# Narrow attention on one Trainium2 core: two heads stacked in 64-row tiles, regrouped loads, splits on GpSimd, division in token layout

## The chip, the cores and the metric

One core of a Trainium2 chip runs the whole program. TensorE (PE) does matmuls from SBUF into the eight banks of PSUM, VectorE (DVE), ScalarE (ACT) and GpSimd (POOL) work on 128 partitions, and SyncE (SP) issues the DMA transfers of this kernel. Each engine runs its own list of instructions in order and waits on semaphores. The metric is the device time of one execution in microseconds.

## What is computed

The reference runs a network of 16 layers on x of 4 x 512 x 128, each added to x after a layer norm. Two layers are "narrow attention": 16 heads of 8 features, without a mask (L0b) and with a causal one (L2b). Cut to what matters:

```python
q = heads(x @ Wq.T + bq); k = heads(x @ Wk.T + bk); v = heads(x @ Wv.T + bv)   # [B, 16, 512, 8]
s = einsum('bhqd,bhkd->bhqk', q, k) * scale          # L2b: -inf where key > query
out = (softmax(s) @ v).reshape(B, 512, 128) @ Wo.T + bo
```

The scores must be as exact as float32. The kernel gets that from bf16 matmuls: q and k are each split into three bf16 parts (value, rest, rest of the rest), and the six products of parts that matter are stacked along the contraction.

## The kernel before

The outer loop runs twice, over two batch elements (b = 0, 1) at a time; the layers stand in it one after the other, each a `Stage` with a list for each engine. Activations are kept feature-major: 128 features on partitions, 512 tokens along a row. `narrow_attention` (L1167) is one stage, so it runs four times: L0b and L2b in each pass.

A stage begins with the layer norm (`Norm`, banks 0 to 3). PE projects q and k (L1260, L1261) and v (L1263) into banks 0, 1, 2, for b = 0 and then for b = 1 into the same banks. DVE adds the biases (L1386, L1387) and splits into parts in five steps (L1389 to L1397) for b = 0, and again for b = 1 after `parted` says that the first parts have left. SP sends the parts of a batch element to memory in one transfer of 128 rows (`send_parts`, L1225) and loads them back (`stack`, L1232, L1233), since the heads must change partitions: operands `qs` and `ks` hold six groups of 8 rows for each head and ones or zeros below; row 48 and the next two of `qs` take the negative row maximum in three parts. Before, one head fills a 128-row operand (only 51 rows are not constant). GpSimd fills `qs` and `ks` whole (L1365), then builds `vpad`, v with a column of ones next to each head (L1367 to L1375).

The work of a stage is cut into 8 units of 4 heads (u = 4b + i). A unit has 17 "top" steps: 16 score tiles (4 heads x 4 query tiles) that PE makes (`top_scores`, L1278, with a mask matmul L1281 in L2b) into banks 4 and 5 in turn, each reduced by DVE to a row maximum (`maxima`, L1403), and a transpose of the maxima (L1273), which DVE negates (L1411) and splits in five more steps (L1413 to L1421). SP puts the three parts into `qs` (L1246) and only then, when they have landed, loads unit u + 2 and waits for it. Units 0 and 1 are loaded ahead (`AHEAD` = 2).

A unit then has 8 slots. In slot s PE makes transposed scores of two heads (`scores`, L1294, mask L1297) into banks 0 and 1 or 2 and 3, ACT takes the exponential of both (L1356) into `pt`, and after each second slot PE multiplies by `vpad` (`products`, L1309; four column tiles of 32) into bank 6 or 7. Between them PE does the tops of later units: `LEAD` = 25 tops run before slot 0, and 17 in each 8 slots afterwards, by `tops_before`. All waits are in the order of the list: a top that must wait for its load (`stacked`) holds up all that follows on PE.

After two units ACT copies a bank of sums (L1349), PE spreads each head's denominator over its 8 rows with a matmul (`spread_den`, L1316), and DVE takes the reciprocal of 128x512 (L1427), multiplies (L1429) and adds v's bias (L1431). The last stretch multiplies by Wo (L1335) for both batch elements and adds to x (L1443).

## Time and profile before

| | us |
|---|---|
| median of 3 runs (lowest, highest) | 3660.25 (3659.43, 3673.93) |
| the profiled execution | 3659.59 |
| its span, from first to last instruction | 3657.6 |
| PE busy | 2741.8 (75%) |
| DVE busy | 1890.3 (52%) |
| ACT busy | 1451.8 (40%) |
| POOL busy | 558.9 (15%) |
| DMA queue of SP | 45.93 MB in 31328 packets, 4.8% of 16 engines' time |

Busy times are sums over the whole span, and a matmul's end is modelled, so a busy PE isn't PE at its peak. They are averages over sixteen layers with different limits; what narrow attention costs is read from windows over its stages and the timeline inside them. The TensorE clock is granted at one of two levels, 1.2 or 2.4 GHz; rows give it as a share of the higher one (0.50 or 1.00), and stretches as a mean.

### The profile page before, as it was taken

What the parts mean: (1) busy time and instruction counts of PE and PEld (TensorE: products, weight loads), DVE (VectorE), ACT (ScalarE), POOL (GpSimd) and SP (SyncE); (2) the same over time, 40 slices, a digit from 0 to 9 for tenths busy, and PEclk for the clock granted to TensorE, in tenths of its full rate; (3) what the DMA queues carried; (4) which work ended last, traced back from release to release, by engine and by line L of the source; (5) the groups of instructions that cost most, each with busy time, mean ns of one, the idle gap of its engine ahead of it and who ended that gap; (6) DMA issues with size and microseconds to landing.
All of it is one profiled execution on the core that took longest, in us unless ns stands there. A gap on an engine that the chain in (4) does not pass through costs nothing. (4 is left out here: it accounts for less than half of the span.)

```text
span 3657.6 us, 33867 instructions
## 1 busy us (share of the span) xinstructions
PE 2741.8 (75%) x12082; PEld 1218.6 (33%) x12082; DVE 1890.3 (52%) x2639; ACT 1451.8 (40%) x2368; POOL 558.9 (15%) x324
## 2 busy tenths in 40 slices
PE   3565769899878579466746657789997877894677
PEld 1221145445344234123212211554443433341232
DVE  4867642455122751595649586415552237416955
ACT  2442511555234244343524424125552433443434
POOL 0533000000003101161006320000000040011600
PEclk8897977999989799799968979689999898997999
DMA  2001000000010210000000020000000102100000
GB/s 91 0 1 39 15 0 1 1 1 1 0 46 1 44 50 6 0 1 1 1 13 0 0 43 11 1 1 1 1 1 0 46 9 41 51 0 0 0 1 6
DMA packets 31504, 48.18 MB, mean 13 GB/s; under 512 B 7520, under 2 KB 19808, under 8 KB 31328
## 3 DMA queue, kind: packets, MB, share of 16 engines
q1 hardware_dynamic: 31328, 45.93, 4.8%
q8 instruction: 98, 1.61, 0.2%
q14 instruction: 78, 0.64, 0.1%
HBM read 38.18 MB, written 7.34 MB: 12 GB/s over the span
## 5 line engine op out<-in xcount | busy, mean ns | idle before, releaser
L1598 ACT ACTIVATE L1b_pr<-ps,L1b_mneg 128x512 f32<-128x512 f32 x256 | 173.8, 684 | 195.7 <-DVE L1b_mneg L1637 195.7
L518 POOL TENSOR_TENSOR xs<-xs,L2f_part 128x512 f32<-128x512 f32 x32 | 40.5, 1264 | 1287.6 <-DVE L2f_part L507 1287.6
L1356 ACT ACTIVATE L0b_pt<-ps 128x1024 f32<-128x1024 f32 x128 | 129.6, 1024 | 209.4 <-PE ps L1294 209.4
L1635 DVE TENSOR_REDUCE L1b_m<-ps 128x2 f32<-128x1024 f32 x128 | 156.7, 1224 | 105.0 <-PE ps L1502 101.0
...
L1403 DVE TENSOR_REDUCE L0b_mx<-ps 128x1 f32<-128x512 f32 x256 | 161.2, 684 | 47.7 <-PE ps L1278 45.0
L1046 POOL TENSOR_TENSOR L0a_db<-L0a_du,L0a_bs 128x1024 f32<-128x1024 f32 x64 | 150.3, 2353 | 227.8 <-ACT L0a_bs L1017 217.1
L1046 POOL TENSOR_TENSOR L3a_db<-L3a_du,L3a_bs 128x1024 f32<-128x1024 f32 x64 | 150.3, 2353 | 226.5 <-ACT L3a_bs L1017 216.0
L1356 ACT ACTIVATE L2b_pt<-ps 128x1024 f32<-128x1024 f32 (+3 forms) x128 | 88.4, 704 | 204.2 <-PE ps L1297 203.7
L1278 PE MATMUL ps<-L0b_ks,L0b_qs 128*128 128x512 bf16 x256 | 104.0, 446 | 87.0 <-DMA L0b_ks<-parts_dram 51.8
L1661 DVE COPY L1b_prt<-ps 128x512 f32<-128x512 f32 x128 | 88.5, 691 | 125.0 <-PE ps L1513 124.7
L1122 DVE TENSOR_TENSOR_SCAN L0a_hs<-ps,L0a_db 128x1024 f32<-128x1024 f32 x64 | 146.1, 2283 | 9.9 <-ACT ps L1009 8.0
L1122 DVE TENSOR_TENSOR_SCAN L3a_hs<-ps,L3a_db 128x1024 f32<-128x1024 f32 x64 | 146.1, 2282 | 9.8 <-ACT ps L1009 8.0
L1403 DVE TENSOR_REDUCE L2b_mx<-ps 128x1 f32<-128x128 f32 (+3 forms) x256 | 116.7, 486 | 54.0 <-PE ps L1281 52.4
L1502 PE MATMUL ps<-L1b_k,L1b_q 64*128 64x512 f32 x512 | 144.0, 640 | 0.0
L1525 PE MATMUL ps<-L1b_prt,L1b_v 128*64 128x512 f32 x512 | 136.7, 614 | 4.1 <-issue 2.0
L1513 PE MATMUL ps<-weights,L1b_pr 128*128 128x128 f32 x1024 | 135.8, 275 | 3.0 <-ACT L1b_pr L1598 3.0
L1278 PE MATMUL ps<-L2b_ks,L2b_qs 128*128 128x128 bf16 (+3 forms) x256 | 80.1, 347 | 76.5 <-DMA L2b_ks<-parts_dram 50.2
L1513 PEld LDWEIGHTS ps<-weights,L1b_pr 128*128 128x128 f32 x1024 | 115.6, 141 | 50.6 <-issue 43.5
L507 DVE SCALAR_TENSOR_TENSOR L2f_part<-ps,weights,L2f_masks 128x512 f32<-128x512 f32 x32 | 24.0, 751 | 205.7 <-PE ps L439 205.7
L946 PE MATMUL ps<-L0a_hc,weights 128*128 128x512 f32 x256 | 127.7, 623 | 2.7 <-DVE L0a_hc L1127 2.7
L507 DVE SCALAR_TENSOR_TENSOR L2g_part<-ps,weights,L2g_masks 128x512 f32<-128x512 f32 x32 | 24.0, 751 | 203.7 <-PE ps L439 203.7
...
## 6 DMA issues: line engine op xcount, KB each, us to landing
...
```

The lines of the kernel that those rows point to most:

```text
L946: mm = pe.matmul(g.ps[:, k, :], g.w("ident"), hc[:, n % 2, k, :], start=(s == 0), stop=(s == NS - 1))
L1046: pool.tensor_tensor(db[:, n % 2, :, :], du[:, b, :, :], bcast(bs[:, n % 2, :], 1, 2), ALU.mult).then_inc(input_ready, 1)
L1122: dve.tensor_tensor_scan(flat(hs), decay_banks(n).rearrange("p k t -> p (k t)"), flat(db), 0.0, ALU.mult, ALU.add).then_inc(scanned, 1)
L1278: mm = pe.matmul(g.ps[:, 4 + a % 2, 0:span(t)], qs[:, b, i, r, t * P:(t + 1) * P], ks[:, b, i, r, 0:span(t)], start=True, stop=not causal)
L1356: act.activation(pt[:, n % 3, 2 * half:2 * half + 2, q0:T], g.ps[:, 2 * (s % 2):2 * (s % 2) + 2, q0:T], ACT.Exp).then_inc(prob, 1)
L1403: dve.tensor_reduce(mx[:, u, n:n + 1], g.ps[:, 4 + a % 2, 0:span(n % 4)], AX.X, ALU.max).then_inc(top_in, 1)
L1502: mm = pe.matmul(g.ps[:, 2 * (s % 2) + h, :], q[HE * h:HE * h + HE, u % 3, t * P:(t + 1) * P], k[HE * h:HE * h + HE, u % 3, :], start=True ...
L1513: mm = pe.transpose(g.ps[:, 4 + h, j * P:(j + 1) * P], pr[:, s % 2, h, j * P:(j + 1) * P], g.w("ident"))
L1525: mm = pe.matmul(g.ps[HE * h:HE * h + HE, PV, :], v[:, u % 4, j, HE * h:HE * h + HE], prt[:, u % 2, h, j, :], start=(j == 0), stop=(j == K ...
L1598: act.activation(pr[:, s % 2, h, :], g.ps[:, 2 * (s % 2) + h, :], ACT.Exp, bias=mneg[:, s % 2, h:h + 1], accum_out=total[:, u % 2, t, h:h ...
L1635: dve.tensor_reduce(m[:, s % 2, :], g.ps[:, 2 * (s % 2):2 * (s % 2) + 2, :], AX.X, ALU.max).then_inc(max_raw, 1)
L1661: dve.tensor_copy(prt[:, u % 2, 0, :, t * P:(t + 1) * P], g.ps[:, 4, :].rearrange("p (j c) -> p j c", c=P)).then_inc(turned_dve, 1)
```

## The change

Two heads share one operand: head 1 on rows 0 to 63, head 2 on rows 64 to 127, 50 rows of each used. `qs` and `ks` become half as large, a score matmul contracts 64 rows, and the two heads of a slot stand in the two halves of the array. The mask matmuls of L2b keep their full height; in `scores` both come after both score matmuls. The negative maximum has two parts instead of three.

Projections of q and k come out with their heads permuted (in `_pack`), b = 1 gets banks of its own (3, 6, 7), and PE starts on b = 0 when its norm is done. DVE splits only b = 0; GpSimd splits b = 1 and, for every unit, the maxima. GpSimd fills `qs` and `ks` through f32 views, and waits for DVE's split before it fills `vpad`.

The parts leave in six transfers for a batch element (part x tensor) into a memory layout of two blocks of 64 rows. A unit's load has again 12 transfers, but with rows of 2 KB and groups of 3, 2 and 1 stacked parts, some of which repeat the source with a step of zero. SP sends the parts of b = 1 after the maxima of unit 0 and ahead of the load of unit 2. `LEAD` is 28. Maxima are collected in an order by halves.

The division moves: PE transposes the copied sums (`turn`), DVE takes reciprocals of 32 columns and multiplies 256, PE transposes back (`turn_back`), and ACT adds the bias (`take_at`). The output of b = 0 moves from the end into slot 41.

The core of the diff:

```diff
-Q_PART = (0, 0, 1, 1, 0, 2)
-K_PART = (0, 1, 0, 1, 2, 0)
+Q_PART = (0, 0, 0, 1, 1, 2)
+K_PART = (0, 1, 2, 0, 1, 0)
...
-    LEAD = 25
+    LEAD = 28
...
+                def send(b, part):
+                    if b == 0:
+                        sp.wait_ge(cut_dve, part + 1)
+                    else:
+                        sp.wait_ge(cut_pool, part + 1)
+                    for x in range(2):
+                        sp.dma_start(g.parts_dram[b, part, x, :, :, :].rearrange("q c t -> c q t"), cut[:, b, part, x, :]).then_inc(sent[part], 16)
+
+                def load(u):
                     b, i = u // 4, u % 4
...
+                    for j, n in ((0, 3), (3, 2), (5, 1)):
+                        for r in range(2):
+                            rows = slice(HALF * r + DH * j, HALF * r + DH * (j + n))
+                            src = g.parts_dram[b, :, :, 16 * i + 8 * r:16 * i + 8 * r + 8, :, :]
+                            sp.dma_start(qs[rows, b, 2 * i:2 * i + 2, :], bcast(src[Q_PART[j], 0], 0, n)).then_inc(stacked, 16)
+                            sp.dma_start(ks[rows, b, 2 * i:2 * i + 2, :], src[K_PART[j]:K_PART[j] + n, 1]).then_inc(stacked, 16)
...
                 for u in range(UN):
...
+                    send_max(u)
+                    if u == 0:
+                        for part in range(PARTS):
+                            send(1, part)
                     if u + AHEAD < UN:
...
+                        load(u + AHEAD)
+                        sp.wait_ge(stacked, (u + AHEAD + 1) * LOADS)
+                    sp.wait_ge(m_rows, 64 * (u + 1))
...
+                    c, t, r = n // 8, n // 2 % 4, HALF * (n % 2)
+                    mm = pe.matmul(g.ps[:, 4 + a % 2, 0:span(t)], qs[r:r + HALF, b, 2 * i + c, t * P:(t + 1) * P],
+                                   ks[r:r + HALF, b, 2 * i + c, 0:span(t)], start=True, stop=not causal)
...
+                    dve.reciprocal(inv[:, :, :], rows[:, :, :, DH]).then_inc(inverse, 1)
...
+                    dve.tensor_tensor(att[:, :, :, 0:DH], rows[:, :, :, 0:DH], bcast(inv[:, :, :], 3, DH), ALU.mult).then_inc(scaled, 1)
...
-        g.parts_dram = nc.dram_tensor("parts_dram", [NB, P, 3, 2, T], BF16, kind="Internal").ap()
+        g.parts_dram = nc.dram_tensor("parts_dram", [NB, 3, 2, P // 2, 2, T], BF16, kind="Internal").ap()
```

SP's queue in the first L0b, from the last load of unit 1 to the first load of unit 2, before (a name is out<-in, then the shape written; waits in brackets):

```order
L1233 DMA L0b_ks<-parts_dram 8x4x512
L1225 DMA parts_dram<-L0b_cut 128x3072 [waits L0b_cuts,L0b_stacked]
L1246 DMA L0b_qs<-L0b_mcut 1x16x128 [waits L0b_m_steps,L0b_ones_in,L0b_parted]
L1246 DMA L0b_qs<-L0b_mcut 1x16x128 x2
L1233 DMA L0b_qs<-parts_dram 8x4x512 [waits L0b_m_rows]
L1233 DMA L0b_ks<-parts_dram 8x4x512
```

and now:

```order
L1236 DMA L0b_ks<-parts_dram 8x1024
L1244 DMA L0b_qs<-L0b_mcut 1x8x128 [waits L0b_m_hi,L0b_stacked]
...
L1244 DMA L0b_qs<-L0b_mcut 1x8x128 [waits L0b_m_lo]
...
L1227 DMA parts_dram<-L0b_cut 2x64x512 [waits L0b_cut_pool]
...
L1227 DMA parts_dram<-L0b_cut 2x64x512 [waits L0b_cut_pool]
...
L1227 DMA parts_dram<-L0b_cut 2x64x512 [waits L0b_cut_pool]
...
L1235 DMA L0b_qs<-parts_dram 24x1x1024
L1236 DMA L0b_ks<-parts_dram 24x1x1024
```

The one 128x3072 transfer of b = 1, which stood ahead of the maxima, is now six of 2x64x512 between the maxima of unit 0 and the load of unit 2.

PE from slot 0 of the first L0b (L1294 is a score, L1278 a top, L1309 products, L1273 the transpose), before:

```order
L1294 MATMUL ps<-L0b_qs,L0b_ks 128x512 [waits L0b_m_rows]
L1294 MATMUL ps<-L0b_qs,L0b_ks 128x512
L1278 MATMUL ps<-L0b_ks,L0b_qs 128x512 [waits L0b_top_in] x3
L1294 MATMUL ps<-L0b_qs,L0b_ks 128x512 x2
L1278 MATMUL ps<-L0b_ks,L0b_qs 128x512 [waits L0b_top_in] x2
L1294 MATMUL ps<-L0b_qs,L0b_ks 128x512 [waits L0b_prob]
L1294 MATMUL ps<-L0b_qs,L0b_ks 128x512
L1309 MATMUL ps<-L0b_pt,L0b_vpad 32x512 [waits L0b_vpad_ready,L0b_prob]
...
L1278 MATMUL ps<-L0b_ks,L0b_qs 128x512 [waits L0b_top_in] x2
L1294 MATMUL ps<-L0b_qs,L0b_ks 128x512 [waits L0b_prob]
...
L1278 MATMUL ps<-L0b_ks,L0b_qs 128x512 [waits L0b_top_in]
L1273 MATMUL ps<-weights,L0b_mx 16x128 [waits L0b_top_in]
```

and now (L1309 a score, L1293 a top, L1327 products, L1288 the transpose):

```order
L1309 MATMUL ps<-L0b_qs,L0b_ks 128x512 [waits L0b_m_rows,L0b_v_in,L0b_proj_in]
L1309 MATMUL ps<-L0b_qs,L0b_ks 128x512
L1293 MATMUL ps<-L0b_ks,L0b_qs 128x512 [waits L0b_top_in] x3
L1309 MATMUL ps<-L0b_qs,L0b_ks 128x512 x2
L1293 MATMUL ps<-L0b_ks,L0b_qs 128x512 [waits L0b_top_in] x2
L1309 MATMUL ps<-L0b_qs,L0b_ks 128x512 [waits L0b_prob]
L1309 MATMUL ps<-L0b_qs,L0b_ks 128x512
L1327 MATMUL ps<-L0b_pt,L0b_vpad 32x512 [waits L0b_vpad_ready,L0b_prob]
...
L1288 MATMUL ps<-weights,L0b_mx 16x128 [waits L0b_top_in]
L1293 MATMUL ps<-L0b_ks,L0b_qs 128x512 [waits L0b_stacked,L0b_top_in]
L1309 MATMUL ps<-L0b_qs,L0b_ks 128x512 [waits L0b_prob]
...
L1293 MATMUL ps<-L0b_ks,L0b_qs 128x512 [waits L0b_top_in] x2
```

The transpose of unit 1's maxima and, right behind it, the first top of unit 2 with its wait for `stacked` now stand in slot 2; before, the transpose ended slot 3, and that top stood in slot 4.

DVE at the end of unit 0's maxima, before:

```order
L1403 TENSOR_REDUCE L0b_mx<-ps 128x1 [waits L0b_top] x16
L1411 TENSOR_SCALAR L0b_mt<-ps 16x128 [waits L0b_top]
L1413 CAST L0b_mcut<-L0b_mt 16x128 [waits L0b_top_in]
L1415 TENSOR_TENSOR L0b_mt<-L0b_mt,L0b_mcut 16x128 [waits L0b_m_steps]
L1417 CAST L0b_mcut<-L0b_mt 16x128 [waits L0b_m_steps]
L1419 TENSOR_TENSOR L0b_mt<-L0b_mt,L0b_mcut 16x128 [waits L0b_m_steps]
L1421 CAST L0b_mcut<-L0b_mt 16x128 [waits L0b_m_steps]
L1403 TENSOR_REDUCE L0b_mx<-ps 128x1 [waits L0b_top] x16
```

DVE now:

```order
L1467 TENSOR_REDUCE L0b_mx<-ps 128x1 [waits L0b_top] x16
L1471 TENSOR_SCALAR L0b_mt<-ps 16x128 [waits L0b_top]
L1467 TENSOR_REDUCE L0b_mx<-ps 128x1 [waits L0b_top] x16
L1471 TENSOR_SCALAR L0b_mt<-ps 16x128 [waits L0b_top]
...
L1471 TENSOR_SCALAR L0b_mt<-ps 16x128 [waits L0b_m_lo,L0b_top]
```

and GpSimd now, in the same stage (fills, one step of the split of b = 1, unit 0's maxima):

```order
L1409 MEMSET L0b_ks 128x4096
L1411 MEMSET L0b_vpad 128x4096 [waits L0b_cut_dve]
...
L1426 CAST L0b_cut<-L0b_ln_sq 128x1024 [waits L0b_proj_in]
L1429 TENSOR_TENSOR L0b_ln_sq<-L0b_ln_sq,L0b_cut 128x1024 [waits L0b_cut_pool]
...
L1435 CAST L0b_mcut<-L0b_mt 16x128 [waits L0b_top_in]
L1437 TENSOR_TENSOR L0b_mt<-L0b_mt,L0b_mcut 16x128 [waits L0b_m_hi]
L1439 CAST L0b_mcut<-L0b_mt 16x128 [waits L0b_m_rest]
```

The five small steps have left DVE, and GpSimd has them behind its split of b = 1.

## Rows read from the trace of the kernel before

**Rows 1.** one row a stretch: length, busy us of each engine (instructions), granted clock, DMA share, GB/s
```profile
271.70:469.70 198.00, 133.02 (x568) 34.97 (x568) 139.61 (x208) 72.77 (x77) 36.88 (x11) 0.86 0.12 25
...
1170.00:1342.80 172.80, 112.21 (x824) 50.58 (x824) 115.87 (x208) 52.15 (x77) 36.85 (x11) 0.85 0.14 29
```

**Rows 2.** the same view, inside the first L0b stage
```profile
331.40:441.40 110.00, 88.81 (x427) 22.08 (x425) 83.89 (x151) 55.04 (x56) 0.00 (x0) 0.95 0.14 22
...
441.40:458.80 17.40, 12.81 (x76) 2.98 (x72) 4.86 (x5) 10.87 (x12) 0.00 (x0) 1.00 0.01 2
...
458.80:469.90 11.10, 6.41 (x10) 2.23 (x10) 5.95 (x5) 0.60 (x1) 0.00 (x0) 0.85 0.00 0
```

**Rows 3.** timeline: start us, length us, engine, line, operation [idle before <-what ended it]
```profile
285.69 7.35 POOL L1365 MEMSET L0b_qs<- 128x8192 bf16 x1
...
287.47 6.11 DVE L1393 CAST L0b_cut<-L0b_ln_xc 128x1024 bf16<-128x1024 f32 x1
...
304.30 0.33 SPq L1233 DMA_DIRECT2D L0b_qs<-parts_dram  x1
...
307.98 0.77 DVE L1393 CAST L0b_cut<-L0b_ln_xc 128x1024 bf16<-128x1024 f32 x1
...
311.90 1.01 PE L1278 MATMUL ps<-L0b_ks,L0b_qs 128*128 128x512 bf16 x2 [25.80 <-DMA L0b_ks<-parts_dram]
```

**Rows 4.** DMA view: a send, 12 loads, three row loads (301:304.3, 304:311.8, 325.5:328.9)
```profile
DMA packets 144, 0.79 MB, mean 238 GB/s; under 512 B 16, under 2 KB 16, under 8 KB 144
...
DMA packets 480, 0.39 MB, mean 50 GB/s; under 512 B 96, under 2 KB 480, under 8 KB 480
...
DMA packets 96, 0.01 MB, mean 4 GB/s; under 512 B 96, under 2 KB 96, under 8 KB 96
```

**Rows 5.** windows of 1 us: 2 KB writes, 1 KB reads twice, 2 KB reads (last columns)
```profile
1837.00:1838.00 1.00, 0.00 (x0) 0.00 (x0) 0.00 (x0) 0.00 (x0) 0.00 (x0) 0.62 0.89 350
...
306.30:307.30 1.00, 0.00 (x0) 0.00 (x0) 0.97 (x2) 0.00 (x0) 1.00 (x2) 0.50 0.31 87
...
308.30:309.30 1.00, 0.00 (x0) 0.00 (x0) 0.96 (x2) 0.00 (x0) 0.71 (x1) 0.50 0.58 66
...
1042.50:1043.50 1.00, 1.00 (x2) 0.50 (x2) 0.28 (x1) 0.37 (x1) 0.00 (x0) 0.50 0.84 313
```

**Rows 6.** timeline of PE, L0b: two products one cycle apart
```profile
428.68 1.06 PE L1309 MATMUL ps<-L0b_pt,L0b_vpad 128*32 128x512 f32 x8
...
432.21 1.07 PE L1309 MATMUL ps<-L0b_pt,L0b_vpad 128*32 128x512 f32 x8
```

**Rows 7.** timeline of PE, L0b: the transpose of the maxima
```profile
424.53 0.27 PE L1273 MATMUL ps<-weights,L0b_mx 128*16 128x128 f32 x1 [0.90 <-DVE L0b_mx L1403]
```

**Rows 8.** timeline of PE, L0b: products after PE had been idle
```profile
380.68 1.94 PE L1309 MATMUL ps<-L0b_pt,L0b_vpad 128*32 128x512 f32 x8
```

**Rows 9.** timeline of ACT, L0b: exponentials of two slots without tops
```profile
448.44 1.94 ACT L1356 ACTIVATE L0b_pt<-ps 128x1024 f32<-128x1024 f32 x2 [0.78 <-PE ps L1294]
```

**Rows 10.** timeline of PE, L1b: full-height and 64-row f32 matmuls
```profile
682.37 1.13 PE L1488 MATMUL ps<-xn,weights 128*128 128x512 f32 x2
...
683.34 1.04 PE L1513 MATMUL ps<-weights,L1b_pr 128*128 128x128 f32 x8
...
684.30 1.13 PE L1502 MATMUL ps<-L1b_k,L1b_q 64*128 64x512 f32 x4
...
685.36 1.08 PE L1525 MATMUL ps<-L1b_prt,L1b_v 128*64 128x512 f32 x4
```

**Rows 11.** groups of instructions by form: out<-in xcount, busy us, mean ns, idle before
```profile
L1427 DVE RECIPROCAL xn<-ps 128x512 f32<-128x512 f32 x16 | 53.7, 3355 | 49.1 <-PE ps L1316 49.1
...
L1666 DVE RECIPROCAL L1b_inv<-L1b_total 128x8 f32<-128x8 f32 x32 | 6.2, 193 | 0.0
```

**Rows 12.** timeline of SP, L2b: row-maxima issues of two units
```profile
1236.18 2.02 SPq L1246 DMA_DIRECT2D L2b_qs<-L2b_mcut  x3
...
1248.42 1.77 SPq L1246 DMA_DIRECT2D L2b_qs<-L2b_mcut  x3
```

More of the change, by code:

```diff
@@ new lines, in send_max @@
+                def send_max(u):
+                    b, i = u // 4, u % 4
+                    for p, ready in enumerate((m_hi, m_lo)):
+                        sp.wait_ge(ready, u + 1)
+                        for r in range(2):
+                            row = HALF * r + ROWS + p
+                            sp.dma_start(qs[row:row + 1, b, 2 * i:2 * i + 2, :].rearrange("o c (t k) -> o (c t) k", k=P),
+                                         mcut[8 * r:8 * r + 8, u % 2, p, :]).then_inc(m_rows, 16)
@@ new lines, in _ @@
+                for part in range(PARTS):
+                    send(0, part)
+                sp.wait_ge(filled, 2)
+                for part in range(PARTS):
+                    sp.wait_ge(sent[part], 32)
+                load(0)
+                sp.wait_ge(stacked, LOADS)
+                load(1)
+                sp.wait_ge(stacked, 2 * LOADS)
+                for u in range(UN):
+                    send_max(u)
+                    if u == 0:
+                        for part in range(PARTS):
+                            send(1, part)
+                    if u + AHEAD < UN:
+                        if u + AHEAD == 4:
+                            for part in range(PARTS):
+                                sp.wait_ge(sent[part], 64)
+                        load(u + AHEAD)
+                        sp.wait_ge(stacked, (u + AHEAD + 1) * LOADS)
+                    sp.wait_ge(m_rows, 64 * (u + 1))
@@ L1434, in _, with output @@
+                def output(b):
+                    dve.wait_ge(out_ready, b + 1)
+                    dve.scalar_tensor_tensor(out=g.xs[:, b, :], in0=g.ps[:, 7, :], scalar=g.w(w + "_bo"), in1=g.xs[:, b, :],
+                                             op0=ALU.add, op1=ALU.add).then_inc(added, 1)
+                for a in range(LEAD):
                     maxima(a // 17, a % 17)
-                for s in range(8 * UN):
+                for s in range(SLOTS):
                     for a in range(tops_before(s), tops_before(s + 1)):
@@ L1438, in _ @@
                     if s % 16 == 4 and s > 16:
-                        normalise(s // 16 - 1)
-                normalise(2 * NB - 1)
-                for b in range(NB):
-                    dve.wait_ge(out_ready, b + 1)
-                    dve.scalar_tensor_tensor(out=g.xs[:, b, :], in0=g.ps[:, b, :], scalar=g.w(w + "_bo"), in1=g.xs[:, b, :],
-                                             op0=ALU.add, op1=ALU.add).then_inc(added, 1)
+                        divide(s // 16 - 1)
+                    if s == 42:
+                        output(0)
+                divide(2 * NB - 1)
+                output(NB - 1)
 def wide_attention(g, name):
@@ L2086, in by_pairs @@
         out = np.zeros((4, 2, 2, 8, 2, m.shape[1]), f)
[L2087 removed]
+        out[:, :, 0] = np.asarray(m).reshape(2, 2, 4, 8, -1).transpose(2, 1, 3, 0, 4)
         return out.reshape(128, -1)
```

275 lines of the change are left out of this document (141 added, 134 removed).

## Prediction, made before the changed kernel had run

> **What bounds the kernel now.** I read the windows over whole stages first, then inside one stage the timeline of PE and DVE, then the DMA view. The change touches only `narrow_attention`, which runs four times: L0b and L2b, in each of two passes of the outer loop. One L0b takes 198.0 us, one L2b 172.8 us [rows 1], together 742 of the 3657.6 us span. The other stages keep their instructions, so I sum differences inside these four against the profiled 3659.6 us (span 3657.6 plus 2.0 around it; the median of the runs is 3660.25, so no correction between them). Inside L0b no engine is full; there are four regimes.
> (a) An opening up to the first score tile: the first matmul on stacked operands starts only at 311.90, after 25.80 us of PE idleness that a DMA ends [rows 3]. Most of it is DVE's six-step split, whose casts take 6.11 us while GpSimd fills `qs` and `ks` (7.35 us a piece) and 0.77 us when it doesn't.
> (b) 53 slots with "tops" (score tiles made only for the maxima) in them, 331.4 to 441.4 [rows 2]. Products start 3.52 to 3.53 us apart (428.68, 432.21) [rows 6]. Two tops (0.43 until the reduce starts), two reduces of 0.62, a wake-up and top of 0.35, a score pair of 0.5 and products of 1.0 make that loop: PE and DVE take turns.
> (c) Slots without tops: two exponentials of 1.94 us together plus 0.78 us waiting for scores, 2.72 us for two slots [rows 9].
> (d) A tail of 11 us [rows 2] with a reciprocal of 3.36 us [rows 11] and output matmuls.
>
> **The change: the loads.** Here lies the decision. A transfer ends with small packets, one for each share it is dealt into. In before, 12 loads of shape 8x4x512 (32 rows of 1 KB each) show 480 packets, 96 of them under 512 B: 384 rows and 8 closing packets for each load. The 128x3072 send shows 144, so 16 closing ones. Three 1x16x128 row loads show 96: 48 rows and 16 each [rows 4]. So a transfer is cut along its outermost dimension of more than one element, into at most 16 shares, and not along its rows. Both sides must be cut alike. The new sends write 2x64x512 into memory: two shares. The new loads read an outer dimension of 3, 2 or 8. Hence all parts of a batch element pass through two of sixteen engines: 3 parts x 2 tensors x 64 rows of 1 KB = 384 packets on each. That the same two serve every send is assumed; rival 1 holds the other reading.
> The Trainium skill ("DMA: Bandwidth & Descriptors", section on why a DMA increments its semaphore by 16) gives it as a rule: the count of engines is the largest up to 16 that divides the slowest dimension of both sides, and the lowest-numbered ones are taken. By that rule the 8 and 16 of the trace come out, and the new sends get 2 engines.
> How long is a 1 KB packet? Nearest are writes of 2 KB rows to memory: 350 GB/s on 16 engines at 0.89 busy, 0.89 x 16 x 2048 / 350000 = 83 ns, so 42 ns for 1 KB if size is all. Reads of 1 KB rows take 0.31 x 16 x 1024 / 87000 = 58 ns in the first microseconds and 0.58 x 16 x 1024 / 66000 = 144 ns when queued [rows 5]. I take 50 ns, nearest to the writes; range 42 to 80, with 144 as the far end. So the parts of one batch element take 384 x 0.050 = 19.2 us, against some 3 us for the 128-row send.
> A load: engine 0 gets 4 x (8 + 8 + 1) = 68 packets of 2 KB. 2 KB reads cost 0.84 x 16 x 2048 / 313000 = 88 ns [rows 5]; since reads slow when queued I take 110: 7.5 us, plus 0.9 to start and 1.2 to be seen, 9.6 us. Before: first issue 304.30 to the first matmul 311.90, 7.6 less 0.1, so 7.5 [rows 3].
>
> **Opening.** GpSimd's fills halve and end before the casts, so DVE has part 0 at 281.9 and part 2 at 286.1 instead of 301.0. But engines 0 and 1 start at 282.8 and end at 302.0; the loads start at 303.2 (before 304.3), the first top at 312.8 (+1.0). LEAD 28 adds three tops of 0.7 us: the first score is 3.1 us late.
>
> **The stall.** SP issues: row maxima of unit 0, the sends of batch element 1, then the load of unit 2, and waits for it. The maxima of unit 0 are ready some 12.5 us after the first top, at 325.3; with GpSimd's three small steps and four issues of 0.59 the sends go out at 327.7. They end at 328.6 + 19.2 = 347.8, and the load queued behind them on the same engines at 347.8 + 7.5 + 1.2 = 356.5. PE wants unit 2's first top (number 34) in slot 2, 5.2 us after the first score at 333.4: 338.6. It is in order, so scores and products stand behind it: 17.8 us. In L2b the slot comes 5.7 us after its first score, the maxima sooner: 19.5 us. After idleness PE is granted the low clock (1.2 GHz): products take 1.94 us instead of 1.06 [rows 6, 8], and a cycle costs 2 us more: +3 for one to two cycles. GpSimd's own split of batch element 1 (five steps from about 295; each moves less than the 16 KB a partition that a fill writes in 7.35 us [rows 3], so 5 us at most) is over by 320 and holds no send up. Behind the waiting SP stand the row maxima of unit 1, 3 us later on, hidden by slots 3 to 7.
>
> **Steady slots.** An f32 matmul stands as two instructions in these rows: one of full height (x2) takes 1.13 us, and two of 64 rows (x4) take 1.13 us together [rows 10], so a score pair costs half: 3.52 - 0.22 = 3.30 us a cycle. The five small DVE steps move away, but before they ran beside products and cost PE nothing beyond the 0.90 us wait for the transpose [rows 7]; with LEAD 28 the transpose stands behind products and that wait goes: that cycle is 2.96. A unit in L0b: 3.30 + 3.30 + 3.90 (one extra top) + 2.96 = 13.5 instead of 15.3 us. 53 slots took 111.1 us; now 51/8 x 13.5 = 86.1, plus 2 x 2.6 for turning, dividing and turning back, plus 2.3 for the first output moved into slot 41: 93.6, a gain of 17.5. Reciprocals of 32 columns instead of 512 lie near the 0.19 us row, not 3.36 [rows 11]. Slots without tops: 13 x 1.24 + 2.1 = 18.2 instead of 17.3, +0.9. Tail: copy 0.7, turn 1.2, divide 0.9, turn back 1.2, bias 0.75, output matmuls 1.9 to 3.6, add 0.85, so 8 instead of 10.9: -2.9.
> L0b: +3.1 + 17.8 + 3 - 17.5 + 0.9 - 2.9 = **+4.4 us**.
> In L2b each top is a 64-row matmul and then a full-height mask. From a full-height f32 matmul to what follows is 683.34 - 682.37 = 0.97 us, from a 64-row pair 685.36 - 684.30 = 1.06 [rows 10]: 0.09 for a change of tiling, at most, and 44 changes a unit are 4 us, nothing if hidden. I take 2. Score pairs give 1.1, the transpose 0.7: a unit 12.4 to 12.5 instead of 12.24 (SP rows 1236.18 to 1248.42) [rows 12]; bounds 12.0, where SP's own loop of 2.4 + 9.6 us stands, and 14.5. 94.7 us become 51/8 x 12.5 + 7.5 = 87.2, -7.5; slots without tops +3.7; tail -1.7.
> The Trainium skill ("TensorEngine Tiling (Array Packing)", key properties) says that a change of mode drains the array, which speaks against this change; by that rule all 4 us would be paid, 13 us more for each L2b. The 0.09 us row doesn't show more.
> L2b: +3.1 + 19.5 + 3 - 7.5 + 3.7 - 1.7 = **+20.1 us**.
> Sum: 2 x (4.4 + 20.1) = +49, 3659.6 + 49 = **3709 us**.
>
> **Rivals.** (1) The sends spread over all engines, as the SBUF side's 128 rows would allow; this ends on the other side. The parts land about 3 us after the last issue, the load takes 7.5: the first score is 12.9 us early, the stall 1 to 3 us, no clock loss. L0b -12.9 + 1.2 - 17.5 + 0.9 - 2.9 = -31.2, L2b -12.9 + 3 - 7.5 + 3.7 - 1.7 = -15.4, twice: 3566 us. For it: no row shows two sides with different outer counts. Against: the 8x4x512 loads had 32 rows on both sides and used 8. It decides by engines: the sum is zero when a batch element's sends take 49/8 = 6.1 us less, 13 us; two engines at 42 ns need 16.
> (2) Packets slower than I take, as queued reads are: each 10 ns is 3.84 us x 2 x 4 stages = 31 us; 80 ns gives 3801, 144 gives about 4000. For it, that the second pair of rows 5 shows just this slowing; against, that those are reads.
> (3) The 64-row bf16 tiles don't overlap, or the change of tiling is paid in full: 0.88 us a unit in each stage, 5.6 x 4 = +22, and +13 x 2 for the drains: 3755.
>
> **Numbers.** Forecast 62%: 3709, own range 3675 to 3755 (42 to 57 ns a packet, steady slots 5 us a stage either way). Rival 1 16%, rival 2 12%, rival 3 10%. The range 3640 to 3800 leaves out rival 1 and a little above. Half a per cent, about what a measurement of this kernel can tell from no change, is 18 us. Faster takes rival 1 and a low tail of the forecast, 0.18; same is the part of the forecast with packets at 42 ns and better slots, 0.15; slower 0.67.
>
> **What would show it.** The six sends of a stage carry 2 closing packets each and engines move under 55 GB/s for about 19 us; PE's row for the first top ends its wait near 25 us as before; one idle time of 16 to 20 us ended by a load stands in each stage in slot 2; score pairs take about 0.4 us for two; GpSimd's three small steps hide; units come 13.5 us apart in L0b. Wrong if sends land in 3 us, if the stall is absent or much longer, or if L2b's units run far from 12.5 us.

## The result, and the profile after

The changed kernel takes 3716.7 us (median of 4 runs, 3697.2 to 3721.1), the kernel before 3659.8 us beside it: ratio 1.014, 95% interval 1.009 to 1.018. It is slower by 1.4%, 57 us, where 49 were forecast. The profiled execution took 3715.9 us with a span of 3714.2.

First the windows over the four stages, columns as in [rows 1]; of before, [rows 1] shows the first two, and the third and fourth are as long, 197.4 and 173.2 us.

```profile
270.31:464.64 194.33, 120.67 (x592) 29.65 (x592) 97.14 (x159) 75.15 (x81) 28.50 (x39) 0.81 0.08 25
1170.05:1378.87 208.82, 158.83 (x848) 56.78 (x848) 78.02 (x159) 55.07 (x81) 28.50 (x39) 0.67 0.07 24
2127.18:2318.80 191.62, 116.79 (x592) 28.61 (x592) 97.13 (x159) 75.17 (x82) 28.51 (x39) 0.83 0.08 26
3019.03:3211.83 192.80, 141.56 (x848) 54.30 (x848) 77.57 (x159) 55.03 (x81) 28.51 (x39) 0.76 0.08 26
```

L0b is 4 to 6 us *shorter* than before, L2b 36 us longer in the first pass and 20 in the second. The granted clock in L2b fell from 0.85 to 0.67 and 0.76. The four stages together give +45.7 us; 10.9 us more lie in stages whose instructions did not change.

The sends and the stall, in the timeline of SP and PE (first L0b, which starts at 270.31):

```profile
280.36 10.55 SPq L1227 DMA_DIRECT2D parts_dram<-L0b_cut  x6
...
299.22 0.76 SPq L1235 DMA_DIRECT2D L0b_qs<-parts_dram  x1
...
308.72 0.61 PE L1293 MATMUL ps<-L0b_ks,L0b_qs 64*128 64x512 bf16 x2 [27.06 <-DMA L0b_ks<-parts_dram]
...
324.44 10.67 SPq L1227 DMA_DIRECT2D parts_dram<-L0b_cut  x6
335.15 2.64 SPq L1235 DMA_DIRECT2D L0b_qs<-parts_dram  x1
...
349.66 0.58 PE L1293 MATMUL ps<-L0b_ks,L0b_qs 64*128 64x512 bf16 x1 [15.31 <-DMA L0b_ks<-parts_dram]
```

SP issues six sends from 280.4 on, and they have landed by 299.2, when it goes on to the load. The same happens again from 324.4, and PE sits idle for 15.31 us until unit 2's load, queued behind them, lands. The DMA view of 280.3 to 299.2 (the six sends), then of 299.2 to 308.65 (one unit's load):

```profile
DMA packets 780, 0.79 MB, mean 42 GB/s; under 512 B 12, under 2 KB 780, under 8 KB 780
...
q1 hardware_dynamic: 780, 0.79, 12.2%
...
DMA packets 244, 0.39 MB, mean 42 GB/s; under 512 B 52, under 2 KB 52, under 8 KB 244
```

12 closing packets for six sends are two each: two engines. Two of sixteen busy is 12.5%; the row says 12.2%. A packet of 1 KB takes 0.122 x 16 x 18.9 / 768 = 48 ns. The load's 52 closing packets are 4 x 3 + 4 x 2 + 4 x 8, as its outermost dimensions of 3, 2 and 8 give.

The issue of 10.67 us isn't even. The first three sends of the second six take 0.55, 0.54 and 0.88 us to issue, the next three 3.22, 2.63 and 2.63, and the first transfer of the load behind them 2.64 (335.15), where 0.76 was enough with nothing ahead of it (299.22). So the full queue of two engines holds SP up as well. From 335.15 to the top that waits, 14.5 us pass, against 9.5 for the load that had the engines to itself.

In L0b products now come 3.30 us apart (3.53 in [rows 6]) and row maxima 13.43 us apart (PE, then SP):

```profile
366.50 1.07 PE L1327 MATMUL ps<-L0b_pt,L0b_vpad 128*32 128x512 f32 x8
...
369.80 1.07 PE L1327 MATMUL ps<-L0b_pt,L0b_vpad 128*32 128x512 f32 x8
...
365.59 2.72 SPq L1244 DMA_DIRECT2D L0b_qs<-L0b_mcut  x4
...
379.02 2.73 SPq L1244 DMA_DIRECT2D L0b_qs<-L0b_mcut  x4
```

In L2b the same issues, 12.24 us apart in [rows 12], stand 20 to 22 us apart and then 13.65; the windows of the same stretch (PEclk is the third number from the right) show why:

```profile
1270.98 2.73 SPq L1244 DMA_DIRECT2D L2b_qs<-L2b_mcut  x4
1291.45 2.73 SPq L1244 DMA_DIRECT2D L2b_qs<-L2b_mcut  x4
1313.63 2.73 SPq L1244 DMA_DIRECT2D L2b_qs<-L2b_mcut  x4
1327.28 2.72 SPq L1244 DMA_DIRECT2D L2b_qs<-L2b_mcut  x4
...
1260.00:1270.00 10.00, 10.00 (x48) 2.87 (x47) 4.19 (x9) 3.25 (x4) 0.00 (x0) 0.50 0.02 7
...
1300.00:1310.00 10.00, 10.00 (x52) 3.51 (x44) 3.85 (x9) 3.08 (x5) 0.00 (x0) 0.50 0.06 18
...
1320.00:1330.00 10.00, 9.82 (x74) 4.05 (x74) 5.26 (x13) 5.08 (x7) 0.98 (x3) 1.00 0.11 31
```

For 64 us after the stall in the first pass PE is busy 10 us of 10 and still granted half its clock (0.50, 1.2 GHz). At full clock it is busy 9.8 of 10: PE, not SP or DVE, bounds L2b now. One unit at full clock, before (between the two issues of [rows 12]) and after:

```profile
1236.18:1248.42 12.24, 10.57 (x97) 4.89 (x97) 8.57 (x23) 5.53 (x8) 0.00 (x0) 1.00 0.21 34
```
```profile
1313.63:1327.28 13.65, 13.47 (x102) 5.54 (x100) 7.89 (x18) 6.06 (x9) 0.98 (x4) 0.99 0.10 31
```

PE was busy 10.57 of 12.24 us and is busy 13.47 of 13.65.

The rows of PE around a mask say what fills it; three of after, then three of before, both at full clock:

```profile
1320.29 0.23 PE L1293 MATMUL ps<-L2b_ks,L2b_qs 64*128 64x128 bf16 x1
1320.45 0.23 PE L1296 MATMUL ps<-cb 128*128 128x128 bf16 x1
1320.61 0.28 PE L1293 MATMUL ps<-L2b_ks,L2b_qs 64*128 64x256 bf16 x1
```
```profile
1237.85 0.23 PE L1278 MATMUL ps<-L2b_ks,L2b_qs 128*128 128x128 bf16 x1
1237.91 0.22 PE L1281 MATMUL ps<-cb 128*128 128x128 bf16 x1
1237.99 0.28 PE L1278 MATMUL ps<-L2b_ks,L2b_qs 128*128 128x256 bf16 x1
```

From a 64-row top to its full-height mask 0.16 us pass, where two full-height tiles stand 0.06 apart; from the mask to the next top 0.16 against 0.08. So a change of tiling costs 0.08 to 0.10 us each way.

### The profile page after: what moved, and what is told of

Read it like the earlier page. It is cut to its first block and busy times, and to the rows that moved or that the text cites. A ratio compares the mean times of both kernels' runs of the same rounds, so it can differ in the third digit from the quotient of the medians.

```text
span 3714.2 us, 34111 instructions
## 1 busy us (share of the span) xinstructions
PE 2804.3 (76%) x12170; PEld 1223.3 (33%) x12178; DVE 1728.4 (47%) x2443; ACT 1464.7 (39%) x2384; POOL 525.5 (14%) x436
## 5 line engine op out<-in xcount | busy, mean ns | idle before, releaser
L1467 DVE TENSOR_REDUCE L2b_mx<-ps 128x1 f32<-128x128 f32 (+3 forms) x256 | 122.8, 490 | 167.9 <-PE ps L1296 162.9
L1293 PE MATMUL ps<-L0b_ks,L0b_qs 64*128 64x512 bf16 x256 | 100.2, 449 | 122.9 <-DMA L0b_ks<-parts_dram 85.4
L1293 PE MATMUL ps<-L2b_ks,L2b_qs 64*128 64x128 bf16 (+3 forms) x256 | 96.3, 376 | 84.5 <-DMA L2b_ks<-parts_dram 82.2
L116 PE MATMUL ps<-xs,weights 128*128 128x512 f32 x128 | 79.6, 754 | 73.4 <-PEq L220 27.4
L946 PE MATMUL ps<-L3a_hc,weights 128*128 128x512 f32 x256 | 131.0, 636 | 2.7 <-DVE L3a_hc L1127 2.7
L946 PE MATMUL ps<-L0a_hc,weights 128*128 128x512 f32 x256 | 126.8, 619 | 2.7 <-DVE L0a_hc L1127 2.7
```

The costliest lines, as they stand in the source:

```text
L946: mm = pe.matmul(g.ps[:, k, :], g.w("ident"), hc[:, n % 2, k, :], start=(s == 0), stop=(s == NS - 1))
L1293: mm = pe.matmul(g.ps[:, 4 + a % 2, 0:span(t)], qs[r:r + HALF, b, 2 * i + c, t * P:(t + 1) * P], ks[r:r + HALF, b, 2 * i + c, 0:span(t)], ...
L1467: dve.tensor_reduce(mx[:, u, col:col + 1], g.ps[:, 4 + a % 2, 0:span(n // 2 % 4)], AX.X, ALU.max).then_inc(top_in, 1)
```

## The experiments

Stage lengths, from windows between the table loads that bound each stage (L0b, L2b of the first pass, then of the second), and medians; "before" ran beside each and took 3659 to 3662 us.

| kernel | L0b | L2b | L0b | L2b | median us | ratio (95%) |
|---|---|---|---|---|---|---|
| before | 198.2 | 173.0 | 197.4 | 173.2 | 3660 | |
| after | 194.3 | 208.8 | 191.6 | 192.8 | 3716.7 | 1.014 (1.009-1.018) |
| spread | 175.1 | 187.1 | 174.5 | 178.1 | 3636.6 | 0.993 (0.990-0.995) |
| order2 | 186.1 | 190.4 | 181.3 | 190.2 | 3667.4 | 1.001 (1.000-1.003) |
| nomask | 194.8 | 178.0 | 194.6 | 188.5 | 3668.0 | 1.001 (1.000-1.002) |
| spread_order_nomask | 170.8 | 161.1 | 167.9 | 160.8 | 3583.0 | 0.978 (0.976-0.980) |
| order2_halfmask | 181.9 | 171.9 | 184.7 | 171.3 | 3631.1 | 0.992 (0.989-0.995) |
| before_nomask | 197.2 | 171.0 | 197.2 | 169.8 | 3656.4 | 0.999 (0.998-1.000) |
| before_two | 227.9 | 215.0 | 226.6 | 214.9 | 3805.5 | 1.039 (1.037-1.041) |
| loads18 | 164.2 | 145.0 | 164.3 | 150.5 | 3542.3 | 0.968 (0.965-0.971) |
| loads18_mask | 164.3 | 159.3 | 164.2 | 159.3 | 3564.1 | 0.974 (0.972-0.977) |
| loads18_halfmask | 164.1 | 148.3 | 164.2 | 149.8 | 3544.4 | 0.967 (0.965-0.969) |
| loads18_lead24 | 163.6 | 165.8 | 163.6 | 165.8 | 3583.6 | 0.979 (0.977-0.981) |
| loads18_dvemax | 168.5 | 147.5 | 168.3 | 146.5 | 3556.3 | 0.971 (0.969-0.973) |

### The sends over sixteen engines: spread

```
-sp.dma_start(g.parts_dram[b, part, x, :, :, :].rearrange("q c t -> c q t"), cut[:, b, part, x, :])
+for c in range(2):
+    sp.dma_start(g.parts_dram[b, part, x, :, c, :], cut[HALF * c:HALF * (c + 1), b, part, x, :])
```

> The changed kernel with one edit: each 2x64x512 send becomes two sends of 64x512, so that the outermost dimension has 64 elements on both sides. Theory A (the time of the sends is set by the two engines they are dealt over): 2 closing packets per send become 16, the 17 us from first send to last landing become 4 to 6 us, the first top matmul comes 11 to 13 us earlier in each of the four stages, and PE's idle time of 15.3 us (L0b) and 14.0 us (L2b) in slot 2 shrinks to 0 to 4 us. That is 4 x (12 + 12) = 96 us less than 3717, so about 3620, and 3590 if the stretch of low granted clock in L2b (60 us of it after the stall in the first pass) is a sequel of the stall. Rival B (the sends are bound by the issue on SP's queue, 10.6 us for six): the new sends issue just as slowly, gain 4 x 5 or less, 3690 or more. On the clock: theory C (low clock in L2b is a sequel of the stall) has units 2 to 4 of L2b at about 13.7 us; rival D (it comes from the work itself: 64-row tops with a full-height mask behind each) has L2b at the low clock for as long as before, units of 20 to 21 us.

Measured 3636.6 us, 80 less than after. The timeline of PE shows the opening 10 us shorter and the stall halved:

```profile
300.22 0.60 PE L1294 MATMUL ps<-L0b_ks,L0b_qs 64*128 64x512 bf16 x2 [17.13 <-DMA L0b_ks<-parts_dram]
...
333.30 0.58 PE L1294 MATMUL ps<-L0b_ks,L0b_qs 64*128 64x512 bf16 x1 [7.57 <-DMA L0b_ks<-parts_dram]
```

Theory A holds in kind; a stall of 6 to 8 us stays because SP still issues twelve sends, at 0.6 us each and 7.5 in all, ahead of the load. The sum closes: SP's issue of the sends is 3.1 us shorter than in the changed kernel, and from the load's first issue to the waiting top 9.8 us pass instead of 14.5; together 7.8 us, and the stall fell by 7.7. The clock went against theory C in the first pass: with the stall at 6 us, L2b's units were still 21.4, 20.5 and 16 us long. In the second they were 21.4 and then 13.8, as in the changed kernel.

### Two engines in the kernel before: before_two

```
-sp.dma_start(g.parts_dram[b], cut[:, :, :, :])                       # 128 rows outermost
+sp.dma_start(g.parts_dram[b].rearrange("q c a x t -> c q (a x t)"), cut[...])   # 2 x 64
```

> The kernel before the change with one part of the change alone: its sends of 128 rows of 6 KB are written as 2x64 rows, so they go over two engines. Theory A (engines decide; 384 KB an engine took 17 us in the changed kernel): the first load comes 14 us later (at +46.5 instead of +32.6 us from the stage's start) and the row maxima of unit 0, which SP issues behind the second send, some 10 us later than that; 4 x 24 = 96 us, 3755. Rival B (the rows of 1 KB of the new sends are what is slow, not the count of engines): 64 packets of 6 KB an engine need 5 us or less, 3660 to 3680.

Measured 3805.5 us, +144. SP's timeline, and the DMA view of the send (300.2 to 317.3):

```profile
300.14 0.67 SPq L1225 DMA_DIRECT2D parts_dram<-L0b_cut  x1
317.28 0.74 SPq L1233 DMA_DIRECT2D L0b_qs<-parts_dram  x1
```
```profile
DMA packets 130, 0.79 MB, mean 46 GB/s; under 512 B 2, under 2 KB 2, under 8 KB 130
...
q1 hardware_dynamic: 130, 0.79, 11.5%
```

128 rows of 6 KB and two closing packets need 17.1 us where [rows 4] had 144 packets done in 3.3; the first load comes 46.4 us after the stage's start, 46.5 were expected. A row of 6 KB takes 0.115 x 16 x 17.1 / 128 = 246 ns, 41 ns a KB. So the count of engines decides, not the length of a row. The rest of the +144 exceeds the 96 expected: the row maxima wait the whole second send (idle time of 12.0 us before the first score), and this kernel's loads, whose memory rows lie in another order, take 10.9 us instead of 7.6. That is a second difference from the kernel before, 3.3 us a load, so the +144 is not the price of the two engines alone; the 17.1 us of the send are.

### The order of the sends: order2

```
 load(1) ... wait
+send(1, 0)
 for u in range(UN):
     send_max(u)
-    if u == 0: send(1, 0); send(1, 1); send(1, 2)
     load(u + AHEAD) ... wait
+    if u < 2: send(1, u + 1)
```

> The changed kernel with only the order of SP's work changed: the sends of batch element 1 leave one part at a time, after load 1, load 2 and load 3, instead of all together ahead of load 2; they still go over two engines. Theory A (the 14 to 15 us stall is the load of unit 2 queued behind 384 packets on the same two engines): PE's idle in slot 2 falls to 0 to 3 us, the first score comes up to 2 us later, the opening stays: 4 x 12 = 48 us less, 3670. If the low clock in L2b is a sequel of the stall, 3640. Rival B (the load is late for another cause, for instance its own 9.5 us): a stall of over 8 us stays in slot 2, 3695 or more.

Measured 3667.4 us, 49 less than after. The stall is gone in slot 2 (the longest idle time that a load ends after the opening is 3.9 us, at unit 4), which shows its cause: the sends ahead of the load. They held it up on their engines and also in SP's own issue, and this edit takes both away at once; spread's sum above parts them. Two of the same sends are now issued in 1.1 us, not 1.8 us each:

```profile
318.68 1.11 SPq L1227 DMA_DIRECT2D parts_dram<-L0b_cut  x2
```

But L2b stood at the low clock from 16 to 111 us of the stage, 54 us past its first score, in both passes, with no idle time over 1 us that a transfer ended in that stretch. So the low clock stands there without the stall.

### The mask behind each top: nomask, before_nomask, order2_halfmask

```
 mm = pe.matmul(ps[:, 4 + a % 2, 0:span(t)], qs[r:r + HALF, ...], ks[r:r + HALF, ...], start=True, stop=...)
-mm = pe.matmul(ps[:, 4 + a % 2, block], eye, mask_qk, start=False, stop=True)
+(nomask, before_nomask: nothing)
+(halfmask: mm = pe.matmul(..., eye[r:r + HALF, :], mask_qk[r:r + HALF, :], start=False, stop=True))
```

> The changed kernel with one part left out: in L2b the causal mask is not added to the score tiles that are made only for the row maxima, so each maximum goes over the whole width of its tile; the mask of the scores themselves stays. Sends and order as they are, so both stalls stay. Theory A (each change between a 64-row tile and a full-height mask costs PE 0.10 us more than in the kernel before: top to mask 0.16 us where before shows 0.06): 16 masks of 0.06 and 32 changes of 0.10 us are gone, 4.2 us of a 13.7 us unit; DVE's 5.8 to 6 us per unit or SP's loop of 12 us become the bound, so units of 12 us at the high clock, and at the low clock 21 us becomes 13 to 15. L2b gets shorter by 6 x 1.7 at the high clock and by up to 25 in the first pass: 3717 - 10 - 30 = 3675 or so. Rival B (the drains are hidden, as the prediction half supposed): L2b within 4 us of before, 3705 to 3717. On the clock: if the low clock comes from the many short matmuls with drains, L2b in the first pass leaves it within 10 us of the stall's end; if it only follows the stall, it stays low as long as before.

> The kernel before the change with one part left out: the causal mask of the tops (maxima over the whole tile). All its tiles there are of full height, so no tiling changes. If a mask between full-height tiles costs only its 0.06 us and PE is not the bound in L2b (7.7 of 10 us busy), the time stays within 6 us of 3660. If the masks themselves were what fills PE, L2b gains 16 x 0.06 = 1 us a unit or more and 3640 or less comes out.

> As order2 (sends of batch element 1 part by part between the loads, over two engines, no stall over 4 us in slot 2), with one more edit in the causal stages: the mask of a top is a 64-row matmul in the same half of the array as the top before it, not a full-height one. Half of the mask is left out by that, so the maxima go over a partly masked tile; the number of matmuls and their columns stay. Theory D1 (what costs is the change of tiling between top and mask, 0.10 us each way at the high clock, and it also keeps the granted clock low: in order2 L2b stays at the low level until 110 us after the stage's start, 50 us past the first score): top to mask falls from 0.16 to 0.06 us, L2b leaves the low level within 20 us of its first score, its units take 12.0 to 12.8 us, the stage 160 to 172 us instead of 190; total 3667 - 2 x 23 = 3620. Rival D2 (the masks as matmuls cost the time and keep the clock low, whatever their height): L2b stays at 185 or more, total 3655 to 3667.

nomask: 3668.0 us, 49 less than after; its profiled execution, 3690.5, was the slowest of its runs and shows L2b 31 and 4 us shorter than after. before_nomask: 3656.4, 5 us less than before, L2b 2.1 and 3.4 us shorter, so masks between full-height tiles cost 2 to 3 us a stage. (The 7.7 of 10 us in its expectation is not what PE does in the slots: a unit at full clock has 10.57 of 12.24, see above. PE had 1.7 us to spare in each.) order2_halfmask: 3631.1, 36 less than order2, L2b 171.9 and 171.3 us. It has as many matmuls and columns as order2 and differs in the height of the masks alone. Its clock left the low level within 7 us of the first score, with dips until 105 us of the stage. D1 is borne out in total; how much of it was the clock and how much the 0.10 us can't be told from this pair.

### All three: spread_order_nomask

> The changed kernel with all three edits: sends as 64x512 pieces, sent part by part between the loads, and the maxima of the causal stages taken without the mask (that part is left out). If the three theories hold, gains add except that the clock's share is had once: 4 x 24 for sends and stall, 20 to 30 for the clock in L2b, 2 x 10 for the drains at the high clock: 3717 - 96 - 25 - 20 = 3576, which is 2.3% below the kernel before. Rival: SP's own loop (loads of 9.5 us and row maxima of 2.4 us, 12 us a unit) becomes the bound and L2b gains nothing from the mask: 3596.

Measured 3583.0 us, 2.2% faster than before, between the two values expected. L2b's units of 12.7 us in the first pass (row maxima issued 84.7, 97.4 and 110.1 us after the start), with waits of 1.0 to 1.7 us for a load at each, say that SP's loop bounds them there, as the rival held.

### Loads over eight to sixteen engines: loads18

```
-g.parts_dram = [NB, 3, 2, P // 2, 2, T]
+g.parts_dram = [NB, 4, 2, 2, 3, 8, 2, T]      # b, unit, half, q or k, part, row, c, t
-sp.dma_start(qs[rows, ...], bcast(src[Q_PART[j], 0], 0, n));  sp.dma_start(ks[rows, ...], src[K_PART[j]:K_PART[j] + n, 1])
+for m in range(j, j + n): sp.dma_start(qs[8 rows of m, ...], src[0, Q_PART[m]])
+sp.dma_start(ks[rows, ...], src[1, K_PART[j]:K_PART[j] + n].rearrange("n q c t -> (n q) c t"))
```

> As spread_order_nomask (3583), with the memory laid out so that the loads of the k parts have 24, 16 or 8 rows outermost and the loads of the q parts 8 each: 18 loads a unit instead of 12, and 4 KB or more of consecutive memory rows dealt over 8 to 16 engines instead of 1 to 3. The sends have 8 rows outermost now. Theory (a load of a unit, 9.5 us, is bound by the 68 packets on its busiest engine): a unit's load takes 6 to 7.5 us, the first top 2 to 3 us earlier in each stage, and L2b's units, which SP's loop of 12 us holds at 12.7, take 11.5 to 12.3: 3583 - 10 - 8 = 3565. Rival (SP's issue of 18 loads at 0.3 us and the way to the first byte take as long): 3578 to 3590.

Measured 3542.3 us, 3.2% faster than before and 41 less than the kernel it grew from, over twice the 18 that were expected. The edit also changes the sends: with 8 rows outermost in memory they go over eight engines, not sixteen (96 closing packets for twelve). SP still issues them in 7.5 us. A unit's load takes 7.4 us instead of 9.5, and as the waits inside L2b went, the granted clock rose from 0.75 and 0.72 to 0.81 and 0.79 (windows over its two L2b stages, and the DMA view of one unit's load):

```profile
1134.47:1279.49 145.02, 108.96 (x720) 36.69 (x720) 73.77 (x159) 54.24 (x82) 28.55 (x39) 0.81 0.13 34
...
2892.50:3043.02 150.52, 112.46 (x720) 37.12 (x720) 73.86 (x159) 54.46 (x82) 28.55 (x39) 0.79 0.13 33
...
DMA packets 360, 0.39 MB, mean 53 GB/s; under 512 B 168, under 2 KB 168, under 8 KB 360
```

168 closing packets are 12 x 8 + 2 x 12 + 2 x 16 + 2 x 8: a load of 24 rows goes over twelve engines, one of 16 rows over sixteen, one of 8 over eight.

### The price of the masks without a stall: loads18_mask, loads18_halfmask

loads18 with the full mask, and with the 64-row one of above.

> As loads18 (3542), with the full-height causal mask of the tops put back, so that the masks are the only difference and neither a two-engine send nor a late load is left. Theory D1 (a full-height mask behind a 64-row top costs 0.10 us each way and holds the granted clock low for a varying time): L2b's units take 13.7 us at the high level instead of 11.1 to 12, and it stays at the low level for 25 us or more past the first score in at least one pass: L2b 165 to 185 instead of 145 and 150.5, total 3542 + 2 x 17 to 2 x 35, so 3575 to 3610; the difference of the order2 pair was 36. Rival (the masks hurt only together with late loads and the stall): within 15 us of 3542.

> As loads18_mask (3564, L2b 159.3 us in both passes with the granted clock at the high level from the first products on), but the mask behind each top is a 64-row matmul in that top's half of the array; half of the mask is left out. As many matmuls and columns, no change of tiling between top and mask. Theory D1 (the change of tiling is what costs at the high clock: 0.10 us each way, 32 a unit, 3.2 us of 13.4): units of 11 to 12.3 us as without masks, L2b 145 to 152, total 3540 to 3552. Rival D2 (the masks themselves cost it): L2b at 157 to 160, total 3560 to 3568.

Measured 3564.1 and 3544.4 us. L2b takes 159.3 us with full-height masks, at the high clock from the first products to the last slots, and 148.3 and 149.8 with 64-row ones, which had some dips of the clock; loads18 without masks took 145.0 and 150.5. So full-height masks cost 10 us a stage, of which 2.6 lie in the opening (28 tops at the low clock) and the rest in the slots; 64-row masks cost nothing that shows. PE's rows of loads18_halfmask:

```profile
1208.77 0.23 PE L1295 MATMUL ps<-L2b_ks,L2b_qs 64*128 64x128 bf16 x1
1208.84 0.22 PE L1298 MATMUL ps<-cb 64*128 64x128 bf16 x1
1208.84 0.28 PE L1295 MATMUL ps<-L2b_ks,L2b_qs 64*128 64x256 bf16 x1
```

0.07 us from top to mask, and the next top, in the other half of the array, starts beside it. D2 is out. The 10 us are the price of leaving the halves as a whole: the change of tiling and the lost overlap with the next top go together, and no run parts them. But D1's second half failed: with the full masks loads18_mask left the low clock at its first products in both passes. On PE it runs the very instructions that order2 does, at the same pace. PE's rows of loads18_mask, then of order2, and the windows that hold the step:

```profile
1187.59 1.94 PE L1329 MATMUL ps<-L2b_pt,L2b_vpad 128*32 128x512 f32 x8
1189.45 0.38 PE L1290 MATMUL ps<-weights,L2b_mx 128*16 128x128 f32 x1
1189.77 0.28 PE L1295 MATMUL ps<-L2b_ks,L2b_qs 64*128 64x128 bf16 x1
...
1188.00:1189.50 1.50, 1.50 (x9) 0.05 (x1) 0.00 (x0) 0.50 (x1) 0.00 (x0) 0.50 0.41 114
1189.50:1191.00 1.50, 1.50 (x14) 0.68 (x10) 0.57 (x2) 0.26 (x1) 0.70 (x2) 0.85 0.09 27
```
```profile
1220.55 1.94 PE L1327 MATMUL ps<-L2b_pt,L2b_vpad 128*32 128x512 f32 x8
1222.41 0.38 PE L1288 MATMUL ps<-weights,L2b_mx 128*16 128x128 f32 x1
1222.73 0.28 PE L1293 MATMUL ps<-L2b_ks,L2b_qs 64*128 64x128 bf16 x1
...
1221.00:1222.50 1.50, 1.50 (x9) 0.09 (x1) 0.00 (x0) 0.46 (x1) 0.00 (x0) 0.50 0.08 21
1222.50:1224.00 1.50, 1.50 (x8) 0.52 (x7) 0.57 (x2) 0.00 (x0) 0.70 (x2) 0.50 0.13 29
```

From the first score to the transpose every row stands at the same distance in both (5.87 us from products' start back to the first score, 1.86 on to the transpose). One is granted the high clock behind it, the other not for 46 us more. The next 46 us of each, loads18_mask first:

```profile
1189.80:1235.80 46.00, 45.55 (x342) 19.21 (x345) 27.30 (x61) 19.89 (x29) 3.92 (x12) 1.00 0.13 34
```
```profile
1222.75:1268.75 46.00, 46.00 (x221) 14.17 (x220) 17.37 (x38) 13.15 (x19) 2.93 (x9) 0.50 0.09 29
```

So the tops with full masks are work on which PE can stay at the low clock, but whether it does is not settled by PE's instructions. What else decides it stays open.

### Two sizes: loads18_lead24, loads18_dvemax

`LEAD = 24` instead of 28; and the three small steps on the maxima issued by DVE instead of GpSimd.

> As loads18, with 24 tops ahead of the first score instead of 28. The opening holds four tops of 0.7 us less at the low clock, -2.8 us a stage; they come back as four tops in slots at 0.3 to 0.4 us each, +1.4; and the row maxima of a unit are ready 2 slots later, 5 us ahead of need instead of 8, which is still as long as the small steps and sends take (about 5 us). So -1.4 us a stage, 3536. Rival (the maxima's rows come too late by then): a wait of 1 to 3 us at each unit's first score, +8 to +20 us a stage, 3575 or more.

> As loads18, with the three small steps on the row maxima (0.28, 0.42, 0.28 us on GpSimd) done by DVE again, right behind the step that reads the transpose. If they ran beside products before and cost nothing there (as the prediction supposed), 3542 within 6 us; if DVE sets the pace with PE in L0b, each unit is 0.6 us longer, 8 x 0.6 x 2 to 4 stages: 3552 to 3561.

LEAD 24: 3583.6 us, +41, in the range of the rival. It holds for L2b alone, which lost 15 to 21 us; L0b gained 0.6. The row maxima land late at most units there (PE, before a unit's first score):

```profile
1181.06 0.61 PE L1309 MATMUL ps<-L2b_qs,L2b_ks 64*128 64x512 bf16 x2 [1.34 <-DMA L2b_qs<-L2b_mcut]
```

and seven waits of 1.1 to 1.8 us, 9 us in all, came with a granted clock of 0.74 instead of 0.81 and 0.79. The small steps on DVE: 3556.3, +14; L0b is 4.1 us longer in both passes (its steady units take 14.09 us instead of 13.43), L2b unchanged within its scatter. That is 8 of the 14; the rest lies outside what the stages show. DVE sets the pace with PE in L0b, so the steps were not free there.

## Why the prediction was right, and where it was not

Terms in us for each stage, predicted and measured in the first and second pass. The measured rows are: stage start to first exponential (1 us behind the first score), the stall, the rest of first to last exponential, and the tail behind it, each against before.

| term | L0b predicted | measured | L2b predicted | measured |
|---|---|---|---|---|
| opening | +3.1 | -1.1, -0.9 | +3.1 | +1.2, +0.2 |
| stall | +17.8 | +15.3, +15.4 | +19.5 | +13.8, +13.8 |
| clock and slots | -13.6 | -17.0, -16.1 | -0.8 | +21.4, +6.1 |
| tail | -2.9 | -1.0, -4.1 | -1.7 | -0.6, -0.6 |
| sum | +4.4 | -3.9, -5.8 | +20.1 | +35.8, +19.6 |

**Two engines.** Right, and it was the step that decided the sign: two closing packets a send, 48 ns a packet where 50 were taken. Rival 1 (all engines) did not occur in the changed kernel; spread then showed its price, 80 us, somewhat short of the 143 that the rival gave, because SP's issue of twelve sends (7.5 us) stays in the opening, 10 us shorter where 16 were meant, and in the stall, which fell by 7.7. The rule of the Trainium skill ("DMA: Bandwidth & Descriptors", section on why a DMA increments its semaphore by 16) held for each shape here: 2, 3, 8, 12 (for 24 rows) and 16 engines.

**Opening.** The first score was put 3 us late and came about when before's did. The parts moved as worked out (first send 10.05 us into the stage; a load of 9.5 us, 9.6 predicted), but the load was issued 2.6 us sooner than the sum had it, and from the first of 28 tops to the first exponential 20.1 us passed where the sum had 25 tops' 19.5 plus 2.1.

**The stall.** Right in place, cause and kind, 2.5 us too long in L0b and 5.7 in L2b: the second sends went out 2 us sooner in the stage and took 17.1 us instead of 19.2, and PE reached the waiting top 6.5 and 8.1 us after the first score instead of 5.2 and 5.7.

**Slots of L0b.** 3.30 us a cycle and 13.43 us a unit are as predicted (3.30, 13.5), and the 53 slots with tops, 93.6 us in the sum, take 93.75 in loads18, where no stall lies in them. The remaining 3 us of gain lie elsewhere: without the stall these slots took 95.1 and 95.3 us, so the low clock behind it cost about 1.4 us and not 3, and the slots without tops became 0.5 us shorter, not 0.9 longer. Inside the unit two errors cancel. The small steps, which I had at nothing, are worth 0.66 us a unit (loads18_dvemax). They are part of the 1.8 us that a unit gained, so score pairs and the wait for the transpose, for which I took all of it, gave only 1.2.

**Slots of L2b.** Here a term failed. The 0.09 us for a change of tiling was right (0.08 to 0.10), but I took 2 us of 4 and had 12.5 us a unit, a little above SP's loop of 12. At the full clock a unit took 13.65, and 13.3 in loads18_mask: PE is full, so most of the changes are paid. The rule of the Trainium skill ("TensorEngine Tiling (Array Packing)", key properties) is that a change of mode drains the array; the rows of the mask agree with it, and the unit came out halfway between my 12.5 and the 14.5 that I weighed by that rule. The step missed was to add up PE in one unit at full clock: 10.57 us busy of 12.24, less 1.1 for the score pairs, plus 44 x 0.09, is 13.4, more than SP's 12. In the sum this came to less than it could. The slots with tops took 93.0 us in loads18_mask against the 87.2 of the sum, but the slots without tops became 0.5 us shorter where I had them 3.7 longer. From first to last exponential loads18_mask needs 104.0 us, 1.4 less than before, where the sum without stall and clock had 3.8 less.

**The clock.** This is the term that was most mis-sized. "+3 for one to two cycles" was enough in L0b. In L2b the low level stayed for 64 us after the stall in the first pass and 22 in the second. Without the stall, first to last exponential took 126.8 and 111.6 us in the changed kernel, against the 104.0 of loads18_mask, which has the same masks and left the low clock at once: about 23 and 8 us where 3 stood. (An estimate: the two kernels also differ in sends and loads.) The two passes differ in little else. The stall isn't needed for it (order2), and what sets its length is open. The four runs of the changed kernel differ by 24 us, and the longer ones have the lower mean clock (0.869 at 3697.2 us, 0.858 at 3721.1).

**Outside the four stages** 10.9 us more were lost at equal instructions; the stretch from L0b to L2b, for instance, took 700.1 us before, 705.4 after, and 700 to 709 in the other kernels; the granted clock there was 0.91 before and 0.89 after. So it is of the size by which this stretch scatters from kernel to kernel; why is open.

So the total of 57 was hit with 49 because L0b's terms were too dear by 18 us and L2b's and the rest too cheap by 26. The place, cause and kind of the stall were foreseen; that the number came so near is in good part luck. L0b was forecast longer and got shorter, and one sign named for being wrong did show: L2b's units ran at 20 to 22 us and at 13.65, far from 12.5.
